# Putting off a correction's weighted addition until the next correction is found, in the scan mixer of a four-layer network kernel

## The reference, cut to what matters

```python
def step(h, x_t):
    h = jnp.clip(h * A[None] + x_t[:, :, None] * Bm[None], -10.0, 10.0)
    y = jnp.einsum('bid,id->bi', h, C)
    return (h, y)
...
A = -jnp.clip(jnp.exp(A_log), -10.0, -0.01)
out_f = _ssm_scan(x_ssm, A, B_mat, C_mat, reverse=False)
out_b = _ssm_scan(x_ssm, A, B_mat, C_mat, reverse=True)
out = (out_f + out_b) * 0.5 * jax.nn.silu(gate)
return jnp.einsum('bli,di->bld', out, out_proj_w)
```

## Time and profile before

| | us |
|---|---|
| median of 3 runs | 3515.78 |
| lowest, highest | 3512.66, 3516.91 |
| the profiled execution | 3514.12 |
| its span, first to last instruction | 3512.4 |
| VectorE busy | 1914.4 (55%) |
| TensorE busy | 2777.3 (79%) |
| share of the span at full TensorE clock, granted | 0.883 |

### The profile page before, as it was taken

The page is one execution under the profiler, slowest core; times in us unless marked ns, Lnnn a source line. Parts: engine busy times, 40 slices in busy tenths (PEclk is TensorE's granted clock), DMA queues, the critical chain, the costliest instruction groups (busy, mean ns, idle before and its releaser), DMA issues. The chain is left out here.

```text
span 3512.4 us, 32400 instructions
## 1 busy us (share of the span) xinstructions
PE 2777.3 (79%) x10146; PEld 1386.7 (39%) x10146; DVE 1914.4 (55%) x3721; ACT 1359.5 (39%) x1987; POOL 924.4 (26%) x606
## 2 busy tenths in 40 slices
PE   2047888999999989999967777785999999288317
PEld 1023444555555544444434444353333333066203
DVE  6545532222222366666454448414777777598686
ACT  1023433111111156666544321243677777243003
POOL 0014563000000000000023220303899999200005
PEclk7568999999999989999978888996999999699558
DMA  2011111000000065555400002111000000100001
GB/s 53 0 31 40 49 58 36 0 0 0 0 0 0 2 154 142 147 138 143 111 0 1 1 25 75 34 52 63 1 1 1 10 1 1 33 1 1 2 0 31
DMA packets 107457, 126.08 MB, mean 36 GB/s; under 512 B 22283, under 2 KB 60300, under 8 KB 107052
## 3 DMA queue, kind: packets, MB, share of 16 engines
q1 hardware_dynamic: 105260, 120.13, 12.9%
q0 software_dynamic: 2048, 4.20, 0.4%
HBM read 108.55 MB, written 14.16 MB: 35 GB/s over the span
## 5 line engine op out<-in xcount | busy, mean ns | idle before, releaser
L2462 PE MATMUL dots_x<-all_xt,delta_wE 128*128 128x512 f32 x768 | 366.9, 614 | 3.5 <-DVE dots_g L2557 2.0
L2447 POOL TENSOR_TENSOR dots_pr<-dots_g 128x512 f32<-128x512 f32 (+2 forms) x96 | 305.7, 3205 | 41.5 <-DVE dots_g L2557 33.7
L1046 DVE SCALAR_TENSOR_TENSOR attn_sim<-attn_sc,attn_mask 128x512 f32<-128x512 f32 (+3 forms) x256 | 125.8, 492 | 316.9 <-PE attn_sc L972 313.8
L972 PE MATMUL attn_sc<-attn_q,attn_xb 128*128 128x512 f32 (+3 forms) x768 | 295.0, 486 | 0.0
L983 PE MATMUL attn_op<-attn_sim,attn_v 128*128 128x512 f32 (+3 forms) x768 | 295.0, 486 | 0.0
L1332 DVE TENSOR_TENSOR grp_h<-grp_sq,grp_cb 128x512 f32<-128x512 f32 x256 | 176.5, 692 | 189.3 <-ACT grp_sq L1220 170.6
L1160 PE MATMUL grp_po<-grp_h,grp_down 128*128 128x512 f32 x512 | 265.2, 600 | 5.8 <-DVE grp_h L1332 5.8
L1152 PE MATMUL grp_ph<-all_xt,grp_up 128*128 128x512 f32 x512 | 263.3, 597 | 0.5 <-ACT grp_sg L1236 0.5
L2554 DVE TENSOR_TENSOR dots_m<-dots_x,dots_sg 128x512 f32<-128x512 f32 x256 | 173.9, 689 | 137.8 <-PE dots_x L2462 131.8
L1214 ACT ACTIVATE grp_r<-grp_ph 128x512 f32<-128x512 f32 x272 | 162.4, 597 | 183.2 <-PE grp_ph L1152 181.6
L2462 PEld LDWEIGHTS dots_x<-all_xt,delta_wE 128*128 128x128 f32 x768 | 136.2, 191 | 235.0 <-issue 140.5
(11 more groups left out here) (623 smaller groups left out, 4876.2 us busy)
## 6 DMA issues: line engine op xcount, KB each, us to landing
grp_cb<-grp_combine SPq DMA_DIRECT2D x512, 128.0 KB, 3.2
mix_cb<-top_weights SPq DMA_DIRECT2D x64, 256.0 KB, 3.2
cap_xs<-cap_zero SPq DMA_DIRECT2D x7, 320.0 KB, 5.1
experts_xe<-cap_xs SPq DMA_DIRECT2D x7, 320.0 KB, 3.3
all_x<-in_L_attn_x_dram SPq DMA_DIRECT2D x4, 512.0 KB, 5.1
cap_w<-in_L_ffn_W_dram SPq DMA_DIRECT2D x1, 2048.0 KB, 8.9
cap_ys<-experts_yo SPq DMA_DIRECT2D x8, 256.0 KB, 2.3
delta_h<-all_xn SPq DMA_DIRECT2D x1, 2048.0 KB
```

Source lines behind the costliest of these rows:

```text
L972: nc.tensor.matmul(sc[k % SC][:, 0:w], xb[:, m * P:(m + 1) * P], q[:, par, n0:n0 + w], start=True, stop=True).then_inc(s_mm, 1)
L2447: nc.gpsimd.tensor_tensor(slot[w % SLOTS][:, at:at + n], a_, b_, ALU.mult).then_inc(pool_ready, 1)
L2462: nc.tensor.matmul(bank(n, sh)[:], wE[:, 1 - k % 2, a, sh], XTj[:, k // 2, par::2], start=True, stop=True).then_inc(u_mm, 1)
```

## The change: what it does

The helper `correct` is split into `correct_chunk` for the first mask and `correct_row` for the second. `correct_row` and its loop do what they did. In `correct_chunk` the weighted addition of a correction is no longer issued behind its own scan. The scan is issued, the place and the number of the correction are written into two registers (`last_at`, `last_n`), and the sequencer goes on to the tests for the next state. When it finds one, it loads the place, waits for the scan, issues the addition that was put off (`apply_last`, with addresses from the two registers), and then the two instructions that write the bounds of the new correction. The first addition of a batch has a weight of zero, for which `nCBS` got one more column; the last one is issued behind the loop. In place of one semaphore that counts 3 for each state there are three (`bounded`, `traced`, `applied`) that count 1 each, so a state or a quad passed over issues three increments.

```diff
-        limS, nCBS = (s.sb(n, [P, NSEG, DS]) for n in ("limS", "nCBS"))
+        limS = s.sb("limS", [P, NSEG, DS])
+        nCBS_all = s.sb("nCBS", [P, NSEG * DS + 1])
+        nCBS = nCBS_all[:, 0:NSEG * DS].rearrange("p (k d) -> p k d", d=DS)
...
-        fix = [s.sem(f"fix{b}") for b in range(BATCH)]
+        fix, bounded, traced, applied = ([s.sem(f"{n}{b}") for b in range(BATCH)] for n in ("fix", "bounded", "traced", "applied"))
...
+                last_at = nc.alloc_register(mybir.EngineType.DVE, "last_at")
+                last_n = nc.alloc_register(mybir.EngineType.DVE, "last_n")
+
+                def apply_last():
+                    g_at = dve.snap(last_at, min_val=0, max_val=NSEG * SEQ - CHUNK)
+                    n_at = dve.snap(last_n, min_val=0, max_val=NSEG * DS)
+                    gk = G_flat[:, bass.ds(g_at, CHUNK)]
+                    return stt(gk, q[:, LEAD:WINDOW, 1], nCBS_all[:, bass.ds(n_at, 1)], gk, ALU.mult, ALU.add)
+
+                def correct_chunk(b, k, d):
                     n = k * DS + d
...
+                    at = dve.value_load(places[0:1, bass.ds(n, 1)], min_val=0, max_val=SEQ - CHUNK)
+                    dve.wait_ge(traced[b], n + 1)
+                    apply_last().then_inc(applied[b], 1)
+                    sk = S_flat[:, bass.ds(k * ROW + at, WINDOW)]
                     L = limS[:].rearrange("p k d -> p (k d)")[:, bass.ds(n, 1)]
...
+                    ts(d1[:, 0:WINDOW, 0], sk, -1.0, L, ALU.mult, ALU.add)
+                    ts(d1[:, 0:WINDOW, 1], sk, L, None, ALU.add).then_inc(bounded[b], 1)
+                    dve.wait_ge(applied[b], n + 1)
+                    dve.wait_ge(bounded[b], n + 1)
+                    nc.vector.tensor_tensor_scan(q[:, 0:WINDOW].rearrange("p t a -> p (t a)"), d0[:, 0:WINDOW].rearrange("p t a -> p (t a)"),
+                                                 d1[:, 0:WINDOW].rearrange("p t a -> p (t a)"), 0.0, ALU.mult, ALU.min).then_inc(traced[b], 1)
+                    dve.reg_mov(last_at, k * SEQ + at)
+                    dve.reg_mov(last_n, n)
...
                 def corrections(b):
-                    dve.sem_inc(apart, 1)
-                    for many in range(2):
+                    def rows(which, body, skip):
                         with dve.Fori(0, NSEG) as k:
...
                                         with dve.If((mask & (1 << d)) > 0):
-                                            correct(b, k, d, many)
+                                            body(b, k, d)
                                         with dve.Else():
-                                            dve.sem_inc(fix[b], 3)
+                                            skip(1)
 
                                     dve.sem_inc(apart, 1)
                                 with dve.Else():
-                                    dve.sem_inc(fix[b], 3 * QUAD)
+                                    skip(QUAD)
+
+                    def skip_chunks(n):
+                        dve.sem_inc(traced[b], n)
+                        dve.sem_inc(applied[b], n)
+                        dve.sem_inc(bounded[b], n)
+
+                    dve.sem_inc(traced[b], 1)
+                    dve.reg_mov(last_at, 0)
+                    dve.reg_mov(last_n, NSEG * DS)
+                    rows(0, correct_chunk, skip_chunks)
+                    dve.wait_ge(traced[b], NSEG * DS + 1)
+                    apply_last().then_inc(applied[b], 1)
+                    dve.wait_ge(applied[b], NSEG * DS + 1)
+                    rows(1, correct_row, lambda n: dve.sem_inc(fix[b], 3 * n))
...
+                c.link(nc.vector.memset(nCBS_all[:, NSEG * DS:], 0.0))
+                c.link(nc.vector.memset(q[:, CT * C:WINDOW], 0.0))
```

More of the change, by code:

```diff
@@ L664, in _ @@
                 tt, ts, stt, redu = nc.vector.tensor_tensor, nc.vector.tensor_scalar, nc.vector.scalar_tensor_tensor, nc.vector.tensor_reduce
-                def correct(b, k, d, many):
-                    n = k * DS + d
[L668 to L677, removed]
-                    L = limS[:].rearrange("p k d -> p (k d)")[:, bass.ds(n, 1)]
-                    w = nCBS[:].rearrange("p k d -> p (k d)")[:, bass.ds(n, 1)]
-                    ts(d1[:, 0:steps, 0], sk, -1.0, L, ALU.mult, ALU.add)
-                    ts(d1[:, 0:steps, 1], sk, L, None, ALU.add).then_inc(fix[b], 1)
+                last_at = nc.alloc_register(mybir.EngineType.DVE, "last_at")
@@ new lines, in correct_row @@
+                def correct_row(b, k, d):
+                    n = k * DS + d
+                    done = n * 3
+                    sk = S_flat[:, bass.ds(k * ROW + LEAD, SEQ)]
+                    gk = G_flat[:, bass.ds(k * SEQ, SEQ)]
+                    L = limS[:].rearrange("p k d -> p (k d)")[:, bass.ds(n, 1)]
+                    w = nCBS_all[:, bass.ds(n, 1)]
+                    ts(d1[:, :, 0], sk, -1.0, L, ALU.mult, ALU.add)
+                    ts(d1[:, :, 1], sk, L, None, ALU.add).then_inc(fix[b], 1)
@@ L682, in correct @@
                     dve.wait_ge(fix[b], done + 1)
-                    nc.vector.tensor_tensor_scan(q[:, 0:steps].rearrange("p t a -> p (t a)"), d0[:, 0:steps].rearrange("p t a -> p (t a)"),
-                                                 d1[:, 0:steps].rearrange("p t a -> p (t a)"), 0.0, ALU.mult, ALU.min).then_inc(fix[b], 1)
+                    nc.vector.tensor_tensor_scan(q[:].rearrange("p t a -> p (t a)"), d0[:].rearrange("p t a -> p (t a)"),
+                                                 d1[:].rearrange("p t a -> p (t a)"), 0.0, ALU.mult, ALU.min).then_inc(fix[b], 1)
@@ L685, in correct @@
                     dve.wait_ge(fix[b], done + 2)
-                    stt(gk, q[:, lead:steps, 1], w, gk, ALU.mult, ALU.add).then_inc(fix[b], 1)
+                    stt(gk, q[:, :, 1], w, gk, ALU.mult, ALU.add).then_inc(fix[b], 1)
                 def scan(b, k):
@@ L746, in corrections @@
                 def corrections(b):
-                    dve.sem_inc(apart, 1)
-                    for many in range(2):
+                    def rows(which, body, skip):
                         with dve.Fori(0, NSEG) as k:
-                            mask = dve.value_load(masks[0:1, many, bass.ds(k, 1)], min_val=0, max_val=2 ** DS - 1)
+                            mask = dve.value_load(masks[0:1, which, bass.ds(k, 1)], min_val=0, max_val=2 ** DS - 1)
                             for quad in range(DS // QUAD):
@@ L754, in corrections @@
                                         with dve.If((mask & (1 << d)) > 0):
-                                            correct(b, k, d, many)
+                                            body(b, k, d)
                                         with dve.Else():
-                                            dve.sem_inc(fix[b], 3)
+                                            skip(1)
                                     dve.sem_inc(apart, 1)
                                 with dve.Else():
-                                    dve.sem_inc(fix[b], 3 * QUAD)
+                                    skip(QUAD)
[11 more added lines that the diff above has]
+                    rows(1, correct_row, lambda n: dve.sem_inc(fix[b], 3 * n))
                 def gated(b):
                     dve.wait_ge(pj_used, 8 * b + 8)
-                    dve.wait_ge(fix[b], 2 * NSEG * DS * 3)
+                    dve.wait_ge(fix[b], NSEG * DS * 3)
                     for ct in range(CT):
```

## The result

| | before | after |
|---|---|---|
| median of 4 runs each, same chip (us) | 3514.22 | 3556.30 |
| lowest, highest | 3508.11, 3516.91 | 3554.72, 3558.53 |
| profiled execution, its span | 3514.12, 3512.4 | 3554.72, 3553.0 |
| share at full TensorE clock | 0.883 | 0.878 |

The ratio is 1.0124 [1.0112, 1.0137]: the change costs 42 us, where 24 were forecast and the range ended at 3551.

The account below looks back on a forecast made before the run. VectorE's work before `y_ready` was taken to bound TensorE in batches 0, 1 and 3, with 3.7 us slack in batch 2. Batches -3.8, +5.8, +15.5, +4.8 sum to +22.3 on 3514.1, plus 1.7: 3538; range 3502 to 3551.

Parts of the forecast that it names:

- the third rival: First walk: a way back loses all blocks, or batches 1 and 3 also have four; another 15 to 30 us, 3560; chance 0.09.
- Batch 0's pairs: Batch 0's first walk: putting additions off makes 27 correction pairs take 106.3 us instead of 121.6; batch 0 gains 14.6.
- Increments and the end of the walk: Empty walks: extra increments and the last addition cost +4.3 in batches 1 and 3, +0.6 in 2; cold fetches +1.5, +0.5.
- the first rival: First walk's loop: code blocks are kept, so nothing is fetched again; -3.4 in all, 3512, within the noise; chance 0.26.
- Eviction in batch 0: Batch 0's first walk: the loop's head is fetched anew on each of three ways back, +10.8 us.
- Eviction in the empty walks: Empty first walks: batch 2's loop copy touches four blocks, +14.9 us; batches 1 and 3 keep to three.
- the price of a way back: Jump to the loop's head: 1.9 us where the block ahead is in, 4.3 where its fetch is still queued.
- The tests named: Trace signs: neighbours 3.0 to 3.2 us apart, scan to addition 1.4 to 1.7, over 4 fetches, empty walks growing.
- The rival that is faster: Batch 0: the covered scan gives -20, blocks are kept, increments are cheaper; together -13, 3503; chance 0.25.

Follow-up runs that it names:

- e1: The changed kernel with the first walk's loop placed at slot 40 of a block, touching three blocks: 3544.51 us, ratio 0.9989 to the kernel before.
- e3: The kernel before with its first walk's loop placed at slot 40, three blocks, as a control: 3554.22 us, ratio 1.0018 to the kernel before.
- e8: The changed kernel with one semaphore counted by 3 in place of three, loops left where they fall: 3512.04 us, ratio 1.0000 to the kernel before.
- e2: The changed kernel with the first walk's loop placed at slot 52, touching four blocks: 3630.66 us, ratio 1.0232 to the kernel before.
- e12: The changed kernel with way-back hint and padded loop of 451 slots, placed at slot 84, reaching a fifth block: 3715.90 against 3545.28 us, ratio 1.0487.
- e7: The changed kernel at slot 52, four blocks, with a way-back hint at the top of each round: 3532.44 us, ratio 1.0056 to the kernel before.
- e9: The changed kernel with way-back hint and padded loop of 451 slots, placed at slot 32, four blocks: 3560.08 us, ratio 1.0134 to the kernel before.
- e5: The changed kernel at slot 40 with one semaphore counted by 3 in place of three: 3493.80 against 3512.77 us for the kernel before, ratio 0.9943.
- e11: The changed kernel with one semaphore, loop at slot 76, three blocks: 3488.29 against 3511.80 us for the kernel before, ratio 0.9935.
- e10: The changed kernel with way-back hint and padded loop of 451 slots, placed at slot 60, ending at 511: 3558.13 us, ratio 1.013.

## Why the prediction was right in direction and wrong in size

Slower, through blocks of code that come again, was forecast, and that is what happened. The size was 42 us and not 24; it is the case of the third rival, "The eviction is worse", at 3560, which had a chance of 0.09. Step by step:

- **Batch 0's pairs** (forecast 106.3 us for 27): 103.7 in e1. The wait and the addresses take 0.18 behind the scan's end, where 0.25 and 0.04 were taken. Including the zero-weight addition, batch 0 gained 17.3 in e1 (17.5 against e3 at the same slot), forecast 14.6, within -20 to 0. Right.
- **Increments and the end of the walk** (forecast +4.3 in batches 1 and 3, +0.6 in batch 2, +1.5 and +0.5 for cold rounds): e1 has +7.6, +1.4 and +3.4. Increments were taken at 0.10 and are 0.095. The empty round grew by 3.43 - 2.67 = 0.76, four of them 3.0, forecast 3.2. The rest of batch 1's is its cold first round, 14.38 in the place of 10.42, inside the 0 to 8 stated; against e3, with 12.18 there, batch 1 has +5.2. Right; e1's sum in the mixer is -5.0 against the kernel before and -8.9 against e3, where the first rival had -3.4.
- **Eviction in batch 0** (+10.8): the scans take 113.4 us from first to last, and 103.7 in e1: +9.7. Right in size for a reason that was partly wrong: 18 fetches in the walk, 3 and then five at each of three ways back, all blocks and not the head alone; but a round of 22 to 32 us has its own work, beside which most of the five fetches lie.
- **Eviction in the empty walks: this step failed, twice over.** First, which batches: by the sentence "By that count batches 1 and 3 start near a block's first slot and keep to three blocks, and batch 2 starts near slot 60 and has four again", +14.9 stood in batch 2 and nothing in 1 and 3. The trace has it the other way round: 3.43 a round in batch 2, 10.7 to 15.7 in batches 1 and 3. The count of 282 was exact and that of the new loop, 338 to 354, had it at its low end; what did not hold was where copies 1 to 3 begin, which was counted from the two fetches of batch 0, with none of the fetches of the other batches set against it. How little it takes can be estimated from the count on record with e8, 18 slots from copy to copy for a loop of 298. For a loop of 338 that is 58, and copies 0 to 2 would begin at 58, 116 and 46: four blocks, four blocks, and in batch 2 an end at 46 + 338 = 384, just inside three, as the trace has it. The prediction's 0 for batch 1 and 60 for batch 2 lie 12 and 14 slots further on. For batch 3 that count already failed in e8, so where its copy begins is not shown. Had batch 2 been hit in their place, 3.7 us of slack would have been spent first; two batches in which TensorE waits already were hit instead.
- Second, **the price of a way back**. It was taken from the one jump of the earlier trace rows (1.9) and one more step of the earlier trace rows (2.4), 4.3 in all, as if the head alone had gone. In fact all five come again: a round goes through four steps of 2.4 to 2.7 and a short one, and takes 10.7 where 3.43 is ordinary: +7.3, and up to +12 in batch 3. In which order the blocks push each other out no trace shows. That a fifth block is not held was taken in the forecast, and nothing in the trace before shows it; e2 and e12 do, with 20 and 21 fetches in the walk of batch 1 where e7 and e9 have 4. With the last, shorter round, the first walk of batch 1 has 16.75 + 10.74 + 10.82 + 8.48 = 46.8 against e1's 25.5, +21.3; that of batch 3 45.3 against 17.8, +27.5. These two are what makes the result. e2 against e1 puts the price on every copy: the steps between the projections are 10.3, 23.0, 26.6 and 26.6 us longer, together 86.5.
- **The tests named** did their work: neighbours are 2.69 apart (3.0 to 3.2 forecast, so too long: the sequencer's tests lie wholly beside the scan); scan to addition 1.54, within 1.4 to 1.7; more than 4 fetches between the first and the last correction (18 in the walk). The growths of the empty walks, 4 to 6 in batch 1 and 15 to 20 in batch 2, came out at 29 (47 against 18 by the rounds) and at 3.
- **The rival that is faster** (3503; its terms, -20 and twice +3, add up to -14 and 3502) needed kept blocks and cheaper registers. With kept blocks e1 is at 0.9989, between it and the first rival; only with one semaphore, e5, is it passed.

What stays open: why the cold first round of batch 1 differs by some us between placings (12.2 in e3, 12.6 in e5, 13.7 in e11, 14.4 in e1, 10.4 before). It lies beside the broadcasts of the earlier trace rows, and no run took those away. Why a hinted branch takes longer stays open too.

## What to carry to other kernels

The loop on the chip had a size limit here, and code put into it cost more than the work that it hides: four blocks of 128 instructions were held, one of them the block fetched ahead, and so this loop should touch three (e1, ratio 0.9989, against 1.0232 for four in e2), or carry the hint at its head if it has to touch four (e7, 1.0056), at the price of slower branches (0.124 us a record in the place of 0.056). Count the loop in the compiled stream, add the slot at which each copy begins (each copy began elsewhere: after the change, batch 1's has rounds of 10.7 and batch 2's of 3.4), and place the head instead of leaving it to chance; one trace of the old kernel did not tell where the new copies would fall. Three semaphores counted the same steps here, and one that counts them together took 0.19 us less per passed step (e5 against e1); this and the placing turned a loss of 42 us into a gain of about 20.

## What the runs showed of the hardware that was not expected

- The blocks of instructions are lost all at once: the loop touches a fourth, and all five are fetched in every round (150 fetches in e2, 90 in e1), the first four 2.4 to 2.7 us apart: an empty round of 3.4 us takes 10.7 and more. 12 slots are 86 us (e1, e2).
- With the way-back hint the block ahead is not fetched while the loop runs (e7: 90 fetches in the place of e2's 150), and the loop's branches take longer: 0.124 us a record in the place of 0.056, 0.44 us in an empty round of four quads, 15.2 us in batch 0.
- Behind work the same fetches cost little: about 3 us at each of the three ways back, in rounds of 22 to 31 us (e1 against after, batch 0: 103.7 and 113.4 from the first to the last scan).
- A semaphore increment by the sequencer has a record of 0.021 us and takes 0.095 of its time (an empty round with eight more is 0.76 longer; pads in e10 stand 0.09 apart).
